# Scores of two graph layers issued together, and label sums with 0/1 masks in fp32r

## The reference

```
layer 0:  q,k,v = x W + b, 8 heads of 32; s = where(adj == 0, -16384, q k^T)
          p = softmax(s); z = v; four times: z = 0.9 p z + 0.1 v
          x = layernorm(x + z)
layer 1:  s = where(adj == 0, -inf, (x Wq)(x Wk)^T / 16)
          x = layernorm(x + softmax(s) (x Wv) Wo + bo)
layer 2:  8 heads again; s = where(adj == 0, -inf, q k^T / sqrt(32))
          x = layernorm(x + (softmax(s) v) Wo + bo)
layer 3:  for label d = 1..4: mask_d = (adj == d)
          w_d = mask_d / (rowsum(mask_d) + 1e-8)
          out = relu(sum over d of (w_d x) Wd_d + bd)
          r, z = sigmoids of out and x;  n = tanh(out Wni + r (x Wnh + b) + b)
          x = layernorm((1 - z) n + z x)
```

## Time and profile before

| | us |
|---|---|
| median of three runs (1780.1 to 1781.58) | 1781.53 |
| the profiled execution | 1783.61 |
| its span, first to last instruction | 1781.8 |
| TensorE busy | 1728.4 |
| ScalarE busy | 1190.9 |
| VectorE busy | 1102.2 |
| GpSimd busy | 793.9 |

### The profile page before, as it was taken

One profiled execution on the slowest core, in us unless ns is written; L12 is line 12 of the kernel. 1 busy time (PEld: TensorE's weight loads), 2 busy tenths in 40 slices (PEclk: granted clock), 3 DMA queues, 4 the chain that ended last, 5 costly groups with the idle time before them and its releaser, 6 DMA issues.

```text
span 1781.8 us, 48249 instructions
## 1 busy us (share of the span) xinstructions
PE 1728.4 (97%) x17680; PEld 1549.8 (87%) x17680; DVE 1102.2 (62%) x2741; ACT 1190.9 (67%) x4008; POOL 793.9 (45%) x774
## 2 busy tenths in 40 slices
PE   5799999999999999999999999999999999999995
PEld 4688899998899998899998899998899998889885
DVE  3665666665666665666665666665666666666662
ACT  4576777666777666776666776666777666677652
POOL 1354444444444444444444544444544454544441
PEclk8999999999999999999999999999999999999998
DMA  5000011000000000001001011000011000000000
GB/s 182 27 22 25 20 31 31 17 27 29 18 29 29 20 22 29 18 29 29 23 18 29 18 29 29 27 14 29 18 29 29 29 12 29 19 28 21 13 16 13
DMA packets 70982, 49.39 MB, mean 28 GB/s; under 512 B 4368, under 2 KB 69904, under 8 KB 70288
## 3 DMA queue, kind: packets, MB, share of 16 engines
q1 hardware_dynamic: 70928, 48.66, 9.1%
HBM read 40.26 MB, written 8.39 MB: 27 GB/s over the span
## 4 chain that ended last, share of the span: by engine, by line
PE 93%; issue 2%; DVE 2%; ACT 2%; POOL 1%; DMA 0%; SPq 0%; POOLq 0%; DVEq 0%
PE bank_A L375 15%; PE bank_B L375 10%; PE bank_A L409 7%; PE bank_A L602 6%; PE bank_A L424 5%; PE bank_B L593 5%; PE bank_A L593 5%; PE bank_B L424 4%; PE bank_C L418 3%; PE bank_X L387 3%; PE bank_X L375 3%; PE bank_C L375 3%; PE bank_B L387 2%; PE bank_X L520 2%; PE bank_A L563 2%
## 5 line engine op out<-in xcount | busy, mean ns | idle before, releaser
L802 POOL TENSOR_TENSOR E<-E,rsum 128x512 f32<-128x512 f32 x256 | 266.4, 1041 | 565.3 <-DVE rsum L898 420.2
L810 POOL TENSOR_TENSOR rstd<-var,minus_half 128x2 f32<-128x2 f32 x128 | 92.4, 722 | 283.2 <-DVE var L933 277.4
L409 PEld LDWEIGHTS bank_A<-kT,qT 32*128 32x128 f32 x1024 | 123.2, 186 | 36.4 <-issue 27.1
L680 ACT ACTIVATE vnat<-bank_A 128x256 f32<-128x256 f32 x96 | 36.9, 384 | 170.0 <-PE bank_A L486 169.9
L375 PE MATMUL bank_A<-xT_hi,w_hi 128*128 128x256 f32 x512 | 138.8, 294 | 11.6 <-DVE xT_lo L869 11.6
L409 PE MATMUL bank_A<-kT,qT 32*128 32x128 f32 x1024 | 147.6, 283 | 0.5 <-ACT E L669 0.5
L409 PE MATMUL bank_B<-kT,qT 32*128 32x128 f32 x1024 | 147.6, 283 | 0.0
L375 PE MATMUL bank_A<-xT_hi,w_lo 128*128 128x256 f32 x512 | 132.3, 281 | 0.0
L834 POOL TENSOR_TENSOR E<-E,rcnt 128x512 f32<-128x512 f32 x64 | 78.3, 1245 | 113.7 <-DVE rcnt L1005 113.7
L693 ACT ACTIVATE xT_hi<-bank_A,col 128x256 fp32r<-128x256 f32 x128 | 65.3, 562 | 94.5 <-PE bank_A L393 94.5
L409 PEld LDWEIGHTS bank_B<-kT,qT 32*128 32x128 f32 x1024 | 123.2, 186 | 0.0
(11 more groups left out here) (198 smaller groups left out, 6143.9 us busy)
## 6 DMA issues: line engine op xcount, KB each, us to landing
adj<-in_adj SPq DMA_DIRECT2D x96, 128.0 KB, 2.4
xt_in<-in_xt SPq DMA_DIRECT2D x64, 128.0 KB, 2.2
x_in<-in_x SPq DMA_DIRECT2D x32, 256.0 KB, 2.7
out<-out_sb SPq DMA_DIRECT2D x32, 256.0 KB, 2.2
absent<-in_adj SPq DMA_DIRECT2D x32, 128.0 KB, 2.1
stage<-in_weights SPq DMA_DIRECT2D x3, 1024.0 KB, 10.7
row<-in_rows SPq DMA_DIRECT2D x1, 1152.0 KB, 10.1
stage<-in_l_weights SPq DMA_DIRECT2D x1, 1024.0 KB, 7.5
```

The costliest lines, as they stand in the source:

```text
L409: mm = nc.tensor.matmul(b[:, at:at + P], qT[hs, c, ns], kT[hs, c, ns], start=masked_by is None, stop=masked_by is None or (g, c) == (G - 1 ...
L802: nc.gpsimd.tensor_tensor(e, e, rs[:, part].unsqueeze(2).to_broadcast([P, SB, P]), ALU.mult).then_inc(e_sig.sem, 1)
L810: nc.gpsimd.tensor_tensor(rstd[part][:], var[part][:], minus_half[:], ALU.pow)\
```

## The change

`s0` and `s2` become one step, `s02`: it issues the products of layer 0 for one pair and of layer 2 for the pair two rounds older, block by block in turn, four heads in four row groups and four banks. Layer 2 takes its heads in the order 2, 3, 0, 1 (`HEADS2`), so that its row groups differ from those of layer 0. The second part waits for both layers' first two exp steps. Layer 2's mask matmuls and `no_edge2` go; GpSimd makes `absent2` and VectorE fills the banks with -3e38 (`fill2`), ahead of `max2`. In layer 3 the masks stay 0/1 and are transposed at once, without `wm`; `wT` is fp32r. A label product is copied to a high part (ScalarE, `lab`) and a low part (VectorE, `xlo`); TensorE multiplies both with the mask into the bank that held the product (`agg.0` to `agg.3`, two labels each), VectorE adds each label's sum times 1/count (`acc.0` to `acc.7`), and `out` transposes the result. The last weight load moves behind the first loads of round 1. All lists of steps are new. In the SyncE list layer 2's adjacency waits for `fill2`.

```diff
 ORDER = {
     "tensor": [
-        "ni@4 z@4 k0 q0 v0 s0.0 l1w n1@1 k2@2 wt.0@3 mixt@4 q2@2 vb0 v2@2 g1@1 s0.1 p0.0 n3@3 s2.0@2 vo1@1 wt.1@3",
-        "p0.1 lab.0@3 lab.1@3 s1@1 lab.2@3 lab.3@3 p0.2 s2.1@2 p0.3 out@3 hop0.0 hop0.1 p1@1 p2.0@2 back0.0 back0.1",
-        "p2.1@2 nh@3 hop0.2 hop0.3 o1@1 back0.2 back0.3 p2.2@2 p2.3@2 hop0.4 hop0.5 rh@3 hop2.0@2 back0.4 back0.5",
-        "hop2.1@2 ri@3 hop0.6 hop0.7 wo2.0@2 back0.6 wo2.1@2 n2@1 back0.7",
+        "back0.7@1 agg.1@4 k0 lab.2@4 q0 lab.3@4 k2@2 q2@2 agg.2@4 v2@2 agg.3@4 n1@1 s02.0 out@4 v0 nh@4 vb0 l1w rh@4",
+        "g1@1 ri@4 ni@4 s02.1 p0.0 z@4 p0.1 vo1@1 wt.0@3 p0.2 s1@1 p0.3 mixt@4 p2.0@2 hop0.0 hop0.1 back0.0 p1@1",
+        "back0.1 p2.1@2 hop0.2 hop0.3 n3@3 o1@1 back0.2 p2.2@2 back0.3 p2.3@2 wt.1@3 hop0.4 hop0.5 hop2.0@2 hop2.1@2",
+        "lab.0@3 back0.4 lab.1@3 back0.5 wo2.0@2 agg.0@3 hop0.6 hop0.7 wo2.1@2 back0.6 n2@1",
     ],
     "scalar": [
-        "wt.0@4 g1@2 p0.0@1 hi3@4 t3@4 exp0.2@1 wt.1@4 exp2.0@3 vo1@2 lab.0@4 p0.1@1 lab.1@4 exp2.1@3 exp0.3@1",
-        "split.1@1 exp1@2 lab.2@4 p0.2@1 lab.3@4 exp2.2@3 p0.3@1 split.2@1 exp2.3@3 back0.0@1 out@4 back0.1@1",
-        "split.3@1 p1@2 p2.0@3 p2.1@3 back0.2@1 back0.3@1 p2.2@3 p2.3@3 x0 nh@4 back0.4@1 back0.5@1 split.4@1 r@4",
-        "hi2@2 t2@2 k0 n@4 q0 z@4 v0 hi1@1 t1@1 k2@2 exp0.0 exp0.1 l1w vb0 q2@2",
+        "t2@4 lab.2@6 lab.3@6 k0@2 k2@4 q2@4 q0@2 hi1@3 t1@3 out@6 v0@2 exp0.0@2 exp2.0@4 exp0.1@2 l1w@2 split.1@2",
+        "nh@6 exp2.1@4 r@6 vb0@2 g1@3 x0@1 n@6 p0.0@2 exp0.2@2 z@6 p0.1@2 exp0.3@2 vo1@3 p0.2@2 exp2.2@4 p0.3@2",
+        "split.2@2 exp1@3 exp2.3@4 back0.0@2 back0.1@2 split.3@2 p1@3 p2.0@4 p2.1@4 hi3@5 t3@5 back0.2@2 p2.2@4",
+        "back0.3@2 p2.3@4 wt.0@5 wt.1@5 lab.0@5 back0.4@2 lab.1@5 back0.5@2 split.4@2 hi2@3",
     ],
     "gpsimd": [
-        "e2.0@3 e1@2 ne1@1 e2.1@3 e2.2@3 e2.3@3 sh.1@3 sc.3@5 pow.1@2 ne2@2 absent wm@3 sh.3@5 pow.0@1 pow.2@3 e0.0",
-        "pow.3@4 e0.1 sc.1@2 sc.0@1 sh.0@1 e0.2 e0.3",
+        "e2.0@3 sh.3@6 e0.0@1 e0.1@1 sh.1@3 sh.0@2 e0.2@1 pow.2@4 e0.3@1 e2.1@3 e1@2 pow.3@5 e2.2@3 e2.3@3 absent.2@2",
+        "pow.1@2 ne1@1 sc.3@5 pow.0@1 absent.0 sc.1@2 sc.0@1",
     ],
     "vector": [
-        "y0.1@2 split.3@2 bn.0@2 agg.0@2 eps.0@2 split.4@2 sum@5 lo2@3 bn.2@4 nrm.0@2 agg.2@4 mixa@5 eps.2@4 mixb@5",
-        "mixc@5 fill0.0@1 max0.0@1 nrm.2@4 fill0.1@1 bn.3@5 max0.1@1 l1w@1 lo1@2 rec0.0@1 agg.3@5 eps.3@5 rec0.1@1",
-        "nrm.3@5 v2@3 fill0.2@1 max0.2@1 lo3@4 max2.0@3 max2.1@3 fill0.3@1 max0.3@1 rows@1 rec0.2@1 max1@2 rec0.3@1",
-        "max2.2@3 rec2.0@3 max2.3@3 rec1@2 rec2.1@3 mask@3 hop0.0@1 rec2.2@3 hop0.1@1 split.1@1 o_hi@4 rec2.3@3 cnt@3",
-        "hop0.2@1 hop0.3@1 y1@2 bn.1@2 o_lo@4 hop0.4@1 agg.1@2 hop0.5@1 split.2@1 eps.1@2 guard@3 hop2.0@3 x0",
-        "hop2.1@3 hop0.6@1 nrm.1@2 hop0.7@1 rcnt@3 y2.0@3 y0.0@1 gate@4 y2.1@3",
+        "agg.2@4 fill0.0@1 fill2.0@3 max0.0@1 fill0.1@1 max2.0@3 o_hi@5 max0.1@1 l1w@1 lo1@2 o_lo@5 fill2.1@3",
+        "rec0.0@1 max2.1@3 rec2.0@3 mask@4 gate@5 rec2.1@3 rec0.1@1 sum@5 fill0.2@1 eps.2@4 max0.2@1 fill0.3@1",
+        "fill2.2@3 max0.3@1 rows@1 split.1@1 rec0.2@1 mixa@5 max2.2@3 fill2.3@3 rec0.3@1 mixb@5 mixc@5 max2.3@3",
+        "max1@2 rec2.2@3 bn.3@5 agg.3@5 rec1@2 hop0.0@1 eps.3@5 hop0.1@1 x0 nrm.2@4 nrm.3@5 rec2.3@3 hop0.2@1 cnt@4",
+        "hop0.3@1 lo3@4 guard@4 y1@2 bn.1@2 hop0.4@1 rcnt@4 agg.1@2 eps.1@2 hop0.5@1 split.2@1 hop2.0@3 hop2.1@3",
+        "xlo.0@4 nrm.1@2 xlo.1@4 y2.0@3 acc.0@4 hop0.6@1 hop0.7@1 y0.0@1 acc.1@4 y2.1@3 acc.2@4 acc.3@4 y0.1@1",
+        "split.3@1 lo2@2 xlo.2@4 bn.0@1 agg.0@1 bn.2@3 eps.0@1 split.4@1 xlo.3@4 nrm.0@1 acc.4@4 acc.5@4 v2@2 acc.6@4",
+        "acc.7@4",
     ],
     "sync": [
-        "ld_xt@1 ld_adj.3@4 ld_adj.2@3 ld_adj.1@2 store@6 ld_x@1 ld_adj.0",
+        "ld_x@1 ld_xt ldw@1 ld_adj.3@4 ld_adj.0 store@6 ld_adj.2@2 ld_adj.1",
     ],
 }
...
+
+APART = 2
+EXTRA = {"s02": APART}
+
+HEADS2 = [2, 3, 0, 1]
...
-        wT = sb("wT", [P, G, LABELS, P])
-        xw = sb("xw", [P, G, LABELS, D])
+        wT = sb("wT", [P, G, LABELS, P], F32R)
+        xw = sb("xw", [P, 8 * D])
+        agg = sb("agg", [P, G, D])
...
+        xw_hi = over(xw, "xw_hi", [P, 2, 2, D], F32R)
+        xw_lo = over(xw, "xw_lo", [P, 2, 2, D], F32R, 16 * D)
...
-                    if part == 0:
-                        wait_before(sp, filled0, it, 4)
-                    elif part < 3:
-                        wait_before(sp, (None, ne1_ready, ne2_ready)[part], it, 1)
+                    if part in (0, 2):
+                        wait_before(sp, filled0 if part == 0 else filled2, it, HC)
                     else:
-                        wait_before(sp, masked, it, 1)
+                        wait_before(sp, ne1_ready if part == 1 else masked, it, 1)
...
+                if step == "ldw" and starts(it):
+                    sp.wait_ge(w_split, SPLIT["2"])
+                    load_weights(4)
...
-            def scores(banks, qT, kT, pair, masked_by=None):
-
-                if masked_by is not None:
-                    for b in banks:
-                        nc.tensor.matmul(b[:, :], ident_b[:], masked_by[:].unsqueeze(2).to_broadcast([P, G, NC, P]),
-                                         start=True, stop=False)
+            def scores(runs):
+
                 for g in range(G):
                     for c in range(NC):
                         at, ns = (g * NC + c) * P, slice(g * P, (g + 1) * P)
-                        for j, b in enumerate(banks):
-                            h = 2 * pair + j
-                            hs = slice(h * HD, (h + 1) * HD)
-                            mm = nc.tensor.matmul(b[:, at:at + P], qT[hs, c, ns], kT[hs, c, ns],
-                                                  start=masked_by is None,
-                                                  stop=masked_by is None or (g, c) == (G - 1, NC - 1))
+                        for banks, qT, kT, heads in runs:
+                            for b, h in zip(banks, heads):
+                                hs = slice(h * HD, (h + 1) * HD)
+                                mm = nc.tensor.matmul(b[:, at:at + P], qT[hs, c, ns], kT[hs, c, ns],
+                                                      start=True, stop=True)
                 return mm
 
             def transpose_heads(bank, E, h):
...
+                if step == "s02":
+                    runs, ready = [], []
+                    if exists(it):
+                        if part == 0:
+                            wait(pe, k0_ready, it, 1)
+                            wait(pe, q0_ready, it, 1)
+                        else:
+                            wait(pe, exp0, it, 2)
+                        runs.append((AB0, qT0, kT0, (2 * part, 2 * part + 1)))
+                    it2 = it - APART
+                    if exists(it2):
+                        if part == 0:
+                            wait(pe, q2_ready, it2, 1)
+                            wait(pe, v2_ready, it2, 1)
+                        else:
+                            wait(pe, exp2, it2, 2)
+                        runs.append((AB2, qT2, kT2, HEADS2[2 * part:2 * part + 2]))
+                    scores(runs).then_inc(s02_ready.sem, 1)
...
-                        wait(pe, xw_ready, it, part - 1)
+                        wait(pe, summed_up, it, 2 * (part - 1))
...
+                if step == "agg":
+                    g, pair = divmod(part, LABELS // 2)
+                    wait(pe, xw_lo_ready, it, part + 1)
+                    wait(pe, wt_ready, it, g + 1)
+                    for d in range(2):
+                        for xs in (xw_hi, xw_lo):
+                            mm = nc.tensor.matmul(BA3[part % 2][:, d * D:(d + 1) * D], wT[:, g, 2 * pair + d],
+                                                  xs[:, part % 2, d], start=xs is xw_hi, stop=xs is xw_lo)
+                    mm.then_inc(agg_t.sem, 1)
                 if step == "out":
-                    wait(pe, xw_ready, it, 4)
-                    for c in range(NC):
-                        for g in range(G):
-                            for d in range(LABELS):
-                                mm = nc.tensor.matmul(A3[:, c * GN + g * P:c * GN + (g + 1) * P],
-                                                      xw[:, g, d, c * P:(c + 1) * P], wT[:, g, d],
-                                                      start=d == 0, stop=d == LABELS - 1)
-                    mm.then_inc(out_t.sem, 1)
+                    wait(pe, summed_up, it, G * LABELS)
+                    transpose_y(A3, agg).then_inc(out_t.sem, 1)
                 if step == "nh":
-                    wait(pe, xw_ready, it, 3)
+                    wait(pe, summed_up, it, G * LABELS)
...
+                    if part >= 2:
+                        wait(act, agg_t, it, part - 1)
+                    nc.scalar.activation(xw_hi[:, part % 2].rearrange("p d f -> p (d f)"), BA3[part % 2][:, :],
```

(40 more changed lines are left out.)

92 lines of the change are left out of this document (33 added, 59 removed).

## The result

The changed kernel takes **1821.85 us** (median of four runs, 1820.69 to 1822.87), beside 1781.03 us for the kernel before on the same chip: 1.0228 times as long, 95% interval 1.0215 to 1.0240. The forecast was 1680 and faster. The profiled execution has a span of 1819.8 us and a mean granted clock of 0.961 (before 0.987).

The account below looks back on a forecast made before the run. TensorE, busy for all of a 53.30 us round, was taken as the bound. Its 48.4 us plus 1.4 of waits made 49.8, times 32, plus 76.2 and 10 for fill and drain: 1680 us, range 1635 to 1745.

Parts of the forecast that it names:

- TensorE's sum: TensorE's work a round: 53.30 less 3.24 (joint scores), 1.26 (label sums) and 0.44 (attention steps side by side), 48.4 us.
- Joint step: Two joint score steps a round, four heads running side by side, 1.19 us each: 3.24 us less a round.
- A: In the joint steps the four row groups share something, a group takes a third longer: 1699 us, chance 0.12.
- B: In the joint steps the second pair runs behind the first, +1.72 us a round: 1735 us, chance 0.08.
- E: The joint step joins nothing, the two layers only move: round 51.6 us, time 1737 us, chance 0.02.
- the 1.4 us of waits: Added to each round for TensorE's waits at three tight places, between 0 and 4 us: round 49.8 us.
- The first tight place: From s02.0 to s02.1: TensorE's cover 10.5 us against 10.6 for the chain of exps, taken as equal.
- The second place: From mixt to n3: TensorE's work about 3.6 us, VectorE's about 4.7, a stall near 1 us.
- The third: From hop0.0 to hop0.2: a chain of 2.1 us against 2.1 us of TensorE cover, even.
- C: ScalarE's and VectorE's chains between s02.0 and s02.1 add 2 to 3 us of waits: 1744 to 1776 us, chance 0.14.
- D: VectorE's added 9.05 us lie ahead of steps TensorE waits for, making the kernel slower: middle 1827 us, chance 0.05.
- Fill and drain: Time outside the steady rounds: 76.2 us before, plus 10 for layer 3's longer drain, between 0 and 20.

Follow-up runs that it names:

- e6: The changed kernel with GpSimd's beta adds of layers 0 and 1 moved to the end of its list, nothing left out: 1765.1 us.
- e8: The changed kernel with e1 and e6 together, x0 behind nrm.3 on VectorE and o1 ahead of n3 on TensorE: 1757.5 us.
- e3: The changed kernel with layer 0's products issued ahead of layer 2's in each joint step, two row groups at a time: 1832.7 us.
- e11: e6 with the order of e3, layer 0's products ahead of layer 2's: 1784.9 us.
- e9: The changed kernel with 14 more transposes of the identity on TensorE ahead of p0.2's wait: 1803.9 us.
- e5: The changed kernel with 16 more transposes of the identity on TensorE ahead of p0.3's wait: 1851.7 us.
- e7: The changed kernel without the low halves of the label features, on VectorE and in TensorE's products: 1787.1 us.
- e2: The changed kernel with layer 2's mask fills left out, maxima taken from the unmasked scores: 1802.7 us.
- e12: e8 with layer 3's four 0/1 mask instructions on VectorE moved one round earlier, to the end of its list: 1749.5 us.
- e1: The changed kernel with its two fill values in two tiles of one column each: 1805.0 us.

## Why the prediction was wrong

**TensorE's sum held.** Joint step: forecast 1.1 from its first record to the next step, measured 1.10 to 1.11, with four banks together. Label sums: a part of four matmuls takes 0.48 (933.48 to 933.96), where 0.47 had been worked out. What TensorE issues a round is near the 48.4 us; the records can't confirm it closer than about 0.9 us (e6, at full clock, has it busy for 49.27), and e6 and e8, with the same instructions at full clock, differ by 0.4 in busy time. Rivals A, B and E are refuted by the 1.10, and e3 and e11 add that making the four groups pairs again costs 0.55 a step. The 3.07x of TensorE: Matmul & The Clock Gate (Part 3), from the Trainium skill, is for 512 columns and four matmuls against one at a time; no run here has one at a time, but the third of a matmul that rival A made of it doesn't show: four groups of 128 columns took as long as two.

**The step that failed is the 1.4 us of waits**, under "Capacity is there, so what costs is order". A round was forecast at 49.8 and is 53.81. The 4.0 us are 2.2 of waits beyond the 1.4 (3.57 in all), about 1.0 of clock (an estimate: 0.96 by e6, 0.75 by e9), and 0.9 of TensorE's busy time left over, which e6 keeps. The 0.9 may be short waits under the matmuls' records; no run shows it. Times 32 rounds they are 128 us of the 140 by which the span missed its forecast.

Within that step, three things were off.
- *The prices.* The tight places were summed from one price for each instruction. Some of VectorE's instructions had two lengths already in the trace of before, the adding of eps and the 0/1 masks (ns, minimum, median and maximum):

```profile
L933 DVE TENSOR_SCALAR var<-mv x128: 158/168/979, 52.9 to 1774.6; 128x2 f32<-128x2 f32 x128
```
```profile
L993 DVE TENSOR_SCALAR E<-adj x128: 278/628/1127, 104.9 to 1725.4; 128x256 f32<-128x256 int32 x128
```

  I read groups by their means, as in the earlier trace rows, where neither of these stands, and never laid GpSimd's list beside VectorE's. GpSimd had been written off as "lighter".
- *The place.* The first tight place, from `s02.0` to `s02.1`, held: TensorE waited for the exps at `s02.1` three times in the whole run, 2.4 us. The long wait is in the stretch behind it, from `s02.1` to the third head, `p0.2`, for which the prediction had no sum. Its list of signs named `p0.3`, and the expectations up to e8 repeated it; e5 paid for that. The second place, `n3`, was right and its size too: near 1 us forecast, 34.7 / 32 = 1.1 measured. The third (`hop0.0` to `hop0.2`) hardly showed: 5.7 us in the whole run at `back0` (L507).
- *The clock.* Nothing was set aside for it, because the steady round of before was at 1.00 throughout. A kernel that never waits gives no sign of what a wait costs. The drain of before, with its waits, had a lower clock (0.84 in the earlier trace rows); here the four microseconds behind a wait of 2.2 us have 0.57. e9 shows it from the other side, with more work in less time.

**The rivals on the slow side.** C, fills, maxima and layer 3's work in one queue ahead of `s02.1`, had the size of the waits (2 to 3 us) and half of the mechanism: the queue in front of `rec0.2` is such a one, but one joint step later. At quiet lengths that queue costs little (e6 leaves 0.7 us of wait at `p0.2`), and ScalarE's load had no part in it: its exps were done 0.76 us before `rec0.2`. D said that VectorE's added 9.05 us would land on the path. Its sign came true, with a chance of 0.05, but not its mechanism, and that its middle figure of 1827 lies 5 us from the measured time is luck (a round of 54.4 and 86 us of fill and drain, where 53.8 and 98 were measured): e7 and e2 take 2.9 and 1.7 us of VectorE's time away and the wait remains or falls by a third, e6 takes no instruction away and wins 57 us. No rival had two engines holding each other up.

**Fill and drain**: 76.4 before, 98.0 after, 21.6 more where 10 had been taken and up to 20 allowed. The first and the last start of `vb0` and of `mixt` tell where (min/median/max ns, then these starts):

```profile
L468 PE MATMUL bank_C<-ident,vT x128: 269/273/330, 21.4 to 1638.9; 128*128 128x128 f32 x128
```
```profile
L642 PE MATMUL bank_A<-ident,oT x128: 272/323/476, 204.4 to 1811.1; 128*128 128x128 f32 x128
```

Before, these lines read 22.8 to 1622.9 and 181.8 to 1773.1. From the last pair's `vb0` to its `mixt` it was 150.2 us and is 172.2: 22.0 more for 0.5 us of longer round. The time before the first `vb0` and behind the last `mixt` didn't grow. So it is depth: in a steady round of before `mixt@4` starts 1.85 us ahead of `vb0`, and now 18.0 to 19.1 behind it, 20 us more of a fifth round that each pair takes, and the last pairs walk it with the engines half empty. I had added up the label chain (10 us) and not where `mixt@4` stands in the list. That the term was mis-sized is shown; where it comes from is read off the two spans and the lists, and no run changed the lag alone. Without the low halves (e7) the total is 92.3, so they are some 6 us of it; the other kernels made from the changed one had 95.8 to 103.9. How the rest divides between the label chain and the plain lag was not tried.

All in all the change took 4.9 us of TensorE's work out of a round by the sum, put back 3.6 in waits, about 1.0 in clock and 0.9 of the rest, and added 21.6 us once: 0.52 x 32 + 21.6 = 38 us of span. e12 keeps 2 us of each round and still pays for the depth.

## What to carry to other kernels

Before VectorE gets new work, lay its list beside GpSimd's at the steps that TensorE waits for, and take prices as minimum, median and maximum: two lengths for one instruction meant here that another engine held it up. Where a stall is expected in a kernel that has had none, price the clock as well as the wait. If the sum for the busiest engine is right and the time isn't, look for two lists that meet at a bad place: moving two tokens won 57 us here, leaving out a mask 19. And look at what stands in the list ahead of the small instruction that the next engine needs: here `rec0.2` stood ready to run for 0.76 us behind work of another head and another layer. An earlier place for it was not tried.

## What the runs showed of the hardware

- Fp32 products of 32 rows: sixteen of them (32 records) in four row groups take 1.10 us, as eight in two groups did; issued pair behind pair they take 1.65, less than the 1.10 + 0.86 that I had as the slow bound: the second pair starts before the first is done.
- Some of VectorE's instructions that read SBUF and one of GpSimd in progress ran one after the other, each way round (changed kernel): a 128x2 tensor_scalar from SBUF to SBUF took 0.17 or 1.26 us, a 128x256 mask 0.29 or 1.39, a 128x512 scalar_tensor_tensor of two SBUF operands 0.69 or 1.43, GpSimd's 128x512 scaling 1.04 or 1.40, its beta add 1.26 or 1.74. Not all do: maxima out of a bank kept to 0.65 to 0.69, the batch statistics of an SBUF tile to 0.39 to 0.43 (0.40 to 0.43 in the kernel before), reciprocals of 128x4 to 0.14 to 0.18.
- The predicated copy has a scalar form (0.72 to 0.76 in e1 and e12) when its fill comes from a tile of one column, and a tensor form (0.70, up to 1.74) when it is one column of two.
- With a wait of 2.2 us at `p0.2` and one of 1.1 at `n3` in a round, TensorE's granted clock stood at 1.2 GHz for 2.56 us a round in the mean; with the first at 0.7 us (e6) or filled with work (e9), and the second as before, it stayed at 2.4 GHz in the steady rounds.
